# A message network's two layers on ScalarE: activations dealt alternately, and VectorE's clamp of layer two placed ahead of layer one's product

## The reference, cut to what matters

```python
def mish(x):
    return x * jnp.tanh(jax.nn.softplus(x))
edge_feat = jnp.concatenate([x[src], x[dst], edge_attr], axis=-1)
h = mish(edge_feat @ W1 + b1)
messages = mish(h @ W2 + b2)
agg = jax.ops.segment_sum(messages, dst, num_segments=x.shape[0])
u = mish(jnp.concatenate([x, agg], axis=-1) @ W3 + b3)
out = u @ W4 + b4
```

## Time and profile before

| what | value |
|---|---|
| median of 3 runs | 1639.71 us (1639.4 to 1640.55) |
| the profiled execution | 1639.68 us, span 1638.0 us |
| TensorE, VectorE, ScalarE, GpSimd busy | 95%, 73%, 67%, 41% of the span |
| mean granted clock of TensorE | 0.988 |
| activations of the first layer, each kind | 79 in the span, about 1.06 us each |

### The profile page before, as it was taken

The page is one execution under the profiler, slowest core; times in us unless marked ns, Lnnn a source line. Parts: engine busy times, 40 slices in busy tenths (PEclk is TensorE's granted clock), DMA queues, the critical chain, the costliest instruction groups (busy, mean ns, idle before and its releaser), DMA issues. The chain is left out here.

```text
span 1638.0 us, 25185 instructions
## 1 busy us (share of the span) xinstructions
PE 1549.4 (95%) x8530; PEld 1226.5 (75%) x8530; DVE 1193.1 (73%) x1976; ACT 1097.3 (67%) x1534; POOL 672.7 (41%) x498
## 2 busy tenths in 40 slices
PE   5789899999999999999999999999999999999987
PEld 4765586878788878877854778787878787888774
DVE  8977646555565646465623499999999999999967
ACT  9841546544554546444530599999999999999963
POOL 3410200120012001200302788888888888888601
PEclk9999899999999999999999999999999999999989
DMA  3001320022012201212106767777777777777710
GB/s 106 0 20 66 92 83 26 15 68 87 26 33 84 77 1 33 81 36 78 41 1 222 160 142 148 146 150 150 148 152 148 152 150 148 149 149 150 170 39 32
DMA packets 107048, 153.95 MB, mean 94 GB/s; under 512 B 42043, under 2 KB 47035, under 8 KB 106467
## 3 DMA queue, kind: packets, MB, share of 16 engines
q0 software_dynamic: 72832, 87.84, 28.4%
q1 hardware_dynamic: 34146, 65.21, 12.6%
HBM read 141.02 MB, written 11.73 MB: 93 GB/s over the span
## 5 line engine op out<-in xcount | busy, mean ns | idle before, releaser
L1787 POOL DMA_INDIRECT edge_gathered<-dst_table,edge_index x158 | 262.0, 1658 | 58.7 <-issue 54.4
L223 PE MATMUL edge_z2p<-edge_w_hi,edge_h_hi 128*128 128x512 f32 x628 | 253.3, 403 | 2.6 <-DVE edge_late L2117 2.6
L223 PE MATMUL edge_z2p<-edge_w_lo,edge_h_hi 128*128 128x512 f32 x628 | 249.0, 396 | 0.0
L223 PE MATMUL edge_z2p<-edge_w_hi,edge_h_lo 128*128 128x512 f32 x628 | 248.8, 396 | 0.0
L1756 POOL DMA_INDIRECT edge_gathered<-src_table,edge_index x158 | 201.8, 1277 | 85.4 <-POOL edge_index L1750 30.6
L977 POOL TENSOR_TENSOR h<-h,tr_row_b 128x512 f32<-128x512 f32 x40 | 59.3, 1520 | 271.4 <-ACT C L1222 271.1
L966 POOL TENSOR_TENSOR tr_cw<-w_c,tr_cw 32x1024 fp32r<-32x1024 f32 x7 | 16.6, 2375 | 348.7 <-ACT tr_cw L1182 348.7
L223 PEld LDWEIGHTS edge_z2p<-edge_w_hi,edge_h_hi 128*128 128x128 f32 x628 | 118.4, 189 | 42.0 <-issue 16.9
L223 PEld LDWEIGHTS edge_z2p<-edge_w_hi,edge_h_lo 128*128 128x128 f32 x628 | 118.5, 189 | 28.5
L223 PEld LDWEIGHTS edge_z2p<-edge_w_lo,edge_h_hi 128*128 128x128 f32 x628 | 118.5, 189 | 25.0
L2134 DVE SCALAR_TENSOR_TENSOR edge_early<-edge_early,edge_z1p 128x1024 f32<-128x1024 f32 x79 | 96.4, 1220 | 48.9 <-ACT edge_early L2002 48.8
(11 more groups left out here) (366 smaller groups left out, 4020.0 us busy)
## 6 DMA issues: line engine op xcount, KB each, us to landing
w_c<-in_attr_T SPq DMA_DIRECT2D x78, 128.0 KB, 4.1
agg<-edge_sum_rows POOLq DMA_DIRECT2D x36, 128.0 KB, 10.7
w_a<-in_wv SPq DMA_DIRECT2D x4, 1024.0 KB, 5.3
w_b<-in_wq SPq DMA_DIRECT2D x4, 1024.0 KB, 5.4
w_a<-in_wk SPq DMA_DIRECT2D x4, 1024.0 KB, 7.7
w_b<-in_wo SPq DMA_DIRECT2D x4, 1024.0 KB, 6.8
w_a<-in_m SPq DMA_DIRECT2D x4, 1024.0 KB, 5.4
w_b<-in_m SPq DMA_DIRECT2D x4, 1024.0 KB, 5.5
```

The source lines that it names most:

```text
L223: mm = pe.matmul(out, a, b, start=(n == 0), stop=(n == last))
L1787: pool.indirect_dma_start(out=from_rows[ring][:, j, :].bitcast(F32), out_offset=None, in_=k.dst_table, in_offset=bass.IndirectOffsetOnAxis ...
```

## The change

ScalarE's eight activations of a step are put in another order. Before: e1, log2, sq1, ln1, q1, e2, q2, sq2. After: e1, log2, sq1, e2, ln1, q2, q1, sq2. On VectorE u2 is moved ahead of h1. The waits stay with their instructions and no instruction is added or removed. The same `step` is used in the filling, the loop and the drain.

```diff
@@ -1996,19 +1996,21 @@
                     if on(2):
                         act.wait_ge(S["u1_ready"], s(-1))
                         act.activation(m1[one], m1[one], ACT.Square).then_inc(S["inner1_ready"], 1)
-                        act.wait_ge(S["inner1_ready"], s(-2) * 2 + 1)
-                        act.activation(m1[one], m1[one], ACT.Ln, bias=1.0).then_inc(S["inner1_ready"], 1)
-                        act.wait_ge(S["inner1_ready"], s(-1) * 2)
-                        act.activation(m1[one], m1[one], ACT.Exp, scale=-1.0).then_inc(S["q1_ready"], 1)
                     if on(4):
                         act.wait_ge(S["z2_ready"], s(-4) * PT + (PT if on(3) else 1))
                         if on(6):
 
                             act.wait_ge(S["h2_ready"], s(-5))
                         act.activation(m2[two], z2[two], ACT.Exp).then_inc(S["e2_ready"], 1)
+                    if on(2):
+                        act.wait_ge(S["inner1_ready"], s(-2) * 2 + 1)
+                        act.activation(m1[one], m1[one], ACT.Ln, bias=1.0).then_inc(S["inner1_ready"], 1)
                     if on(5):
                         act.wait_ge(S["log2_ready"], s(-4))
                         act.activation(m2[old], m2[old], ACT.Exp, scale=-1.0).then_inc(S["q2_ready"], 1)
+                    if on(2):
+                        act.wait_ge(S["inner1_ready"], s(-1) * 2)
+                        act.activation(m1[one], m1[one], ACT.Exp, scale=-1.0).then_inc(S["q1_ready"], 1)
                     if on(4):
                         act.wait_ge(S["u2_ready"], s(-3))
                         act.activation(m2[two], m2[two], ACT.Square).then_inc(S["square2_ready"], 1)
@@ -2129,12 +2131,12 @@
...
+                    if on(4):
+                        dve.wait_ge(S["e2_ready"], s(-3))
+                        dve.tensor_scalar(m2[two], m2[two], TOP, 1.0, ALU.min, ALU.add).then_inc(S["u2_ready"], 1)
                     if on(2):
                         dve.wait_ge(S["q1_ready"], s(-1))
                         dve.scalar_tensor_tensor(m1[one], m1[one], 0.5, ps_z1[one][:, :], ALU.subtract, ALU.mult).then_inc(S["h1_ready"], 1)
-                    if on(4):
-                        dve.wait_ge(S["e2_ready"], s(-3))
-                        dve.tensor_scalar(m2[two], m2[two], TOP, 1.0, ALU.min, ALU.add).then_inc(S["u2_ready"], 1)
```

## The result

The changed kernel took 1844.44 us (median of 4 runs, 1842.26 to 1847.24), the kernel before beside it 1639.76. The ratio is 1.125, with a 95% interval of 1.1234 to 1.1267: slower by 204.7 us.

What follows compares the result with a forecast made beforehand. A ScalarE-VectorE ring, 16.69 us for two steps, was taken as the bound, TensorE just keeping up. h1 of step 80 207.2 us late, less 2.5 in the drain: 1639.7 + 204.7 = 1844 us; range 1826 to 1872.

Steps and rivals of the forecast that it cites:

- The ring: VectorE and ScalarE, edge stage: u1, z2, e2, ln1, q2, q1, h1, next u1; two steps 22.18 us, before 16.69.
- From h1 of step 6 to h1 of step 80: Steady edge stage: 37 times two steps at 22.18 us, 820.7 us; h1 of step 80 207.2 us late.
- The filling: First steps of the edge stage: steps 2 and 3 unchanged, h1 of step 6 at 954.4, 5.3 us late.
- The drain: End of the edge stage: shorter by 2.5 us, the middle between 0 and 4.5.
- The backlog: TensorE behind at the drain: z2 waited 1.33 us for it, e2 later 3.16; none with the slower ring.
- e2 waits for z2: ScalarE's e2, due about 1.5 us too early, stops for VectorE's z2 of the same step and starts 0.03 after it.
- u2 ahead of h1: VectorE: u2 leaves the stretch between h1 and hi, so the ring loses its 0.60 us; hi then starts later behind h1.
- rival 1: ScalarE's order: only the slots cost, z2_ready is there in time; 83 us more, 1723 us; chance 0.05.
- The upper bound: ScalarE's three starts from e2 to q1: each 1.09 us instead of 0.96, 29 us more, 1873 us.
- TensorE's clock: TensorE, edge stage: gaps, 5.6 us free in two steps, make falls from the full rate likely; costed at nothing.
- The room of the product: TensorE's second-layer product, odd step: ends 9.4 us after u1, next z2 wants it at 13.0; 3.6 us of room.
- What I said would show it: Edge-stage signs: h1 10.9 and 11.3 us apart, e2 idle about 1.5, TensorE busy about 75%, waiting for z2 or h1.

Runs made afterwards that it cites:

- The run of the two slots without the wait: Changed kernel with e2 moved two places back, behind ln1 and q2 and still ahead of q1: 1740.16 us, ratio 1.0615.

## Why the prediction was right, point by point

The forecast was 1844 us; the median came out at 1844.44. The mechanism is the forecast one, but that the numbers meet so closely is luck: the profiled execution took 1842.26 us, 2.1 less than the forecast's terms give (0.9 of it lie ahead of the stage's first h1, at 916.29 and not 917.23), and the four runs spread over 5 us. The terms one by one, against the profiled execution:

- *The ring* was forecast at 22.18 us for two steps; in the middle of the stage it is 11.26 + 10.95 = 22.21 from h1 to h1. Single terms were off and cancel: u1 to the end of z2 in the odd step took 3.24 (1399.93 to 1403.17) instead of 3.41, since u1 takes 0.69 there and not 0.88; h1 to the next u1 took 4.05 and 3.55 instead of 3.96 and 3.51, since hi starts 1.35 behind h1 and not 1.26 (in the 3.55 the attributes' high part gives half of this back); the even step's e2 came some 0.1 later. Up to step 15 the 1.26 of the filling still holds in the changed kernel, and two steps take about 21.9 us there.
- *From h1 of step 6 to h1 of step 80* 820.7 us were forecast; it is 1772.81 - 953.41 = 819.4.
- *The filling* put h1 of step 6 37.15 us behind h1 of step 2; it is 37.12 (916.29 to 953.41).
- *The drain* was forecast 2.5 us shorter, taken as the middle between 0 and 4.5. From h1 of step 80 to the end of the span it is 1840.6 - 1772.81 = 67.8 us instead of 1638.0 - 1567.92 = 70.1: 2.3 shorter. The size is right by luck. The backlog that the forecast named gives only 0.7: e2 of step 81 comes 6.46 us after h1 of step 80 instead of 7.17, and its wait for z2 is longer than before (4.46 us instead of 3.16), not gone. The other 1.6 come from a later wait of VectorE for TensorE, which the forecast did not have; the kernel before and the changed one:

```profile
1587.18 0.69 DVE L2164 COPY edge_early<-edge_z1p 128x512 f32<-128x512 f32 x1 [3.06 <-PE edge_z1p L215]
...
1789.73 0.69 DVE L2166 COPY edge_early<-edge_z1p 128x512 f32<-128x512 f32 x1 [1.42 <-PE edge_z1p L215]
```

- *e2 waits for z2* and starts 0.03 behind it: 1403.17 and 1403.20, as in the earlier trace rows. Its idle time is 1.49 and 1.68 us in the odd and the even step, forecast 1.5.
- *u2 ahead of h1* takes its time out of the ring: shown by the run without it (1882 us). That u2 could only go there because e2 moved too was in the working only by half; the run of VectorE's part alone shows it.
- *Slots and wait.* The forecast did not split the 205 us in its text, but rival 1 did, with 83 us for the slots alone. The run of the two slots without the wait measured 102. Its two steps take 19.38 us instead of that rival's 18.93: h1 to the next u1 0.42 more, sq1 to q1 0.11 more in each step (3.95, 1406.20 to 1410.15, since ln1 stands behind sq1 again), u1 to sq1 some 0.18 less in the odd one; 37 x 0.45 = 17 us are the difference between 83 and 102, within 2. Rival 1 as a whole falls: z2_ready is not in time.
- *Two slips in the text.* The starts of h1, given as 10.9 and 11.3 us apart, are the sums from u1 to u1; from h1 to h1 the same terms give 10.83 and 11.35, and 10.95 and 11.26 were measured. The upper bound was worked out as 1873 us, and the range says 1872.
- *TensorE's clock* falls again and again, as expected, and costs nothing. The granted clock is 0.91 in the stretch of 100 us, and 0.65 in the 3 us from 1399, in which a wait of 1.85 us for the attributes' low part ends. The room of the product was smaller than forecast: the last matmul of the burst ends at 1409.95 + 0.40 = 1410.35, 10.4 after u1 and not 9.4 (the sum takes 2.57 us at the low clock and not 1.95, and the matmuls start 0.23 apart, not 0.22), which leaves 2.4 us to z2 at 1412.77 instead of 3.6. The Trainium skill, "TensorE: Matmul & The Clock Gate", section "HAM oscillation — how this bites in real kernels", has a burst after a long wait start cold every time round. The trace agrees in the odd step shown, for the short matmuls and the sum but no longer for the 24 matmuls behind them (0.23 us apart), and not in the even one behind it, where the wait is 1.49 us (before the burst at 1413.50) and the stretch from 1411 to 1414 us keeps 1.00. That it matters for the time is refuted here by the run with more matmuls (1843.8 us at a higher granted clock).
- *What I said would show it* was wrong in two details. TensorE was said to be busy about 75% of the stage; the row says 85.3, since matmuls at the low clock take longer and count as busy. An estimate from the row: a granted clock of 0.91 as a mix of the two levels is about 18 of 100 us at the low one, in which 9 us of work take 18, so 75 becomes 84. And TensorE was said to wait for z2 or h1; it does wait for z2 in the even steps, but in the odd steps for the low part of the attributes (L2155), which VectorE makes behind lo. I had left this wait out of TensorE's schedule; it came at no price, since the products still had room. Both waits, of the odd step and of the even one behind it:

```profile
1399.95 0.58 PE L1869 MATMUL edge_z1p<-edge_attr_parts,edge_attr_w_both 128*128 128x256 f32 x1 [1.85 <-DVE edge_attr_parts L2155]
...
1413.50 0.50 PE L223 MATMUL edge_z2p<-edge_w_hi,edge_h_hi 128*128 128x512 f32 x1 [1.49 <-DVE edge_late L2119]
```

## What to carry to other kernels

In a loop in which two engines hand work to and fro, write down the ring: the instructions that each wait for the one before, through both engines' queues, back to the same instruction one step later. An instruction of another chain that is put between two members of the ring costs its slot at each step (here 0.95 us, of which the stall between dependent neighbours that goes gives back only 0.13), even if the engine has idle time elsewhere; and before any instruction is moved ahead, look up in which step its operand is made and how much cover its wait had (here 0.64 us, with 2.2 us of work taken from in front of it). How busy an engine is does not say whether it sets the pace: add work to it, and see whether the time follows. In the changed kernel TensorE was busy 85%, and none of the added 69 us came through. In the kernel before it was busy 99.9% and had 0.10 us of room in two steps; 64 us came through, so this test alone cannot tell an engine that leads from one that only just keeps up.

## What the hardware showed that was not expected

- On VectorE an instruction that reads what the one before writes starts later, and how much later is not one number. h1 and the instruction behind it stand 1.14 us apart where they are independent (1408.73 to 1409.87 in the run of ScalarE's half alone) and 1.26 where hi follows in the filling of the kernel before. In the changed kernel it is 1.25 to 1.26 in steps 2 to 15, which are written out, and 1.34 to 1.36 (1395.88 to 1397.23, say) from step 16, the first of the loop, to the end of the stage, in the drain too. The three other runs with hi directly behind h1 over the whole stage change at the same step. What makes the difference is open.
- TensorE lost its full clock in the stretch around a gap of 1.85 us in one step and kept it around a gap of 1.49 us in the next. Four more matmuls in a step, 0.93 us of 11, raised the mean granted clock from 0.958 to 0.985 in the profiled executions (0.975 to 0.977 in the other runs).
